# In the last group of an attention kernel, the extra norm tile's statistics move one unit up and its modulation and low part one unit down

## The reference

```
sa, ca, ga, sb, cb, gb = mod            # rows of silu(c) @ wmod; |ga| and |gb| at least 0.25
h = layernorm(x) * (1 + ca) + sa
x1 = x + ga * attention(h)              # 32 q heads, 8 kv heads of 128, rope, causal, window of 128
h = layernorm(x1) * (1 + cb) + sb
out = x1 + gb * ((silu(h @ w1.T + b1) * (h @ w2.T + b2)) @ w3.T + b3)
```

## Time and profile before

| | us |
|---|---|
| median of 3 runs | 1498.3 |
| profiled execution | 1499.11 |
| its span | 1497.3 |
| TensorE busy | 1474.5 (98%) |
| VectorE busy | 1102.8 (74%) |
| GpSimd busy | 863.2 (58%) |
| ScalarE busy | 823.0 (55%) |

### The profile page before, as it was taken

The page is one execution under the profiler, slowest core; times in us unless marked ns, Lnnn a source line. Parts: engine busy times, 40 slices in busy tenths (PEclk is TensorE's granted clock), DMA queues, the critical chain, the costliest instruction groups (busy, mean ns, idle before and its releaser), DMA issues.

```text
span 1497.3 us, 27356 instructions
## 1 busy us (share of the span) xinstructions
PE 1474.5 (98%) x7589; PEld 1227.1 (82%) x7589; DVE 1102.8 (74%) x1852; ACT 823.0 (55%) x2183; POOL 863.2 (58%) x887
## 2 busy tenths in 40 slices
PE   7899999999999999999999999999999999999999
PEld 4578888888888888888888888888888888877887
DVE  6687786877787878788787878787877868783542
ACT  3465655656555656555565655565665556552331
POOL 2356466656565556669855646655664665676333
PEclk9999999999999999999999999999999999999999
DMA  9011110110201111324302020111111101153001
GB/s 317 21 37 57 36 56 28 38 53 7 84 7 56 35 56 35 127 62 128 99 27 66 7 82 9 56 35 56 35 56 35 56 28 35 64 183 127 28 29 57
DMA packets 99216, 90.20 MB, mean 60 GB/s; under 512 B 5466, under 2 KB 73314, under 8 KB 99174
## 3 DMA queue, kind: packets, MB, share of 16 engines
q1 hardware_dynamic: 98582, 88.50, 18.8%
q10 hardware_dynamic: 432, 0.66, 0.1%
q0 software_dynamic: 160, 0.52, 0.1%
HBM read 74.98 MB, written 14.69 MB: 60 GB/s over the span
## 4 chain that ended last, share of the span: by engine, by line
PE 91%; DVE 4%; POOL 2%; issue 1%; ACT 1%; DMA 0%; DVEq 0%; POOLq 0%; ACTq 0%
PE pP L276 11%; PE pP L278 11%; PE pP L277 11%; PE pOp L276 8%; PE pOp L278 8%; PE pOp L277 8%; PE pS L278 4%; PE pS L277 4%; PE pAv L276 4%; PE pS L276 4%; PE pAv L278 4%; PE pAv L277 4%; PE pTr L286 3%; PE pXx L355 1%; POOL pm L1256 1%
## 5 line engine op out<-in xcount | busy, mean ns | idle before, releaser
L1256 POOL TENSOR_SCALAR_AFFINE_SELECT pm<-pT 128x512 fp32r<-128x512 f32 x480 | 393.3, 852 | 474.4 <-DVE pT L868 474.2
L276 PE MATMUL pP<-hT,wp 128*128 128x512 f32 (+1 forms) x776 | 315.1, 406 | 4.7 <-DVE hT L1001 4.0
L278 PE MATMUL pP<-hT,wp 128*128 128x512 f32 (+1 forms) x776 | 303.7, 391 | 0.0
L277 PE MATMUL pP<-hT,wp 128*128 128x512 f32 (+1 forms) x776 | 302.8, 390 | 0.0
L630 ACT CAST oT<-pAv 128x512 fp32r<-128x512 f32 x128 | 74.8, 585 | 280.9 <-PE pAv L278 280.9
L1269 POOL TENSOR_TENSOR rB<-rB,tab 128x512 f32<-128x512 f32 x160 | 218.4, 1377 | 17.3 <-ACT rB L653 17.3
L642 ACT ACTIVATE pr<-pS,nb 128x128 f32<-128x128 f32 x512 | 181.4, 371 | 64.3 <-DVE nb L888 64.3
L898 DVE TENSOR_TENSOR rA<-pP,tab 128x512 f32<-128x512 f32 x160 | 110.2, 689 | 130.8 <-ACT rB L653 130.8
L276 PE MATMUL pOp<-wos,oT 128*128 128x512 f32 x512 | 201.4, 393 | 4.0 <-DVE oT L863 3.8
L278 PE MATMUL pOp<-wos,oT 128*128 128x512 f32 x512 | 199.5, 390 | 0.0
L277 PE MATMUL pOp<-wos,oT 128*128 128x512 f32 x512 | 199.4, 389 | 0.0
(11 more groups left out here) (196 smaller groups left out, 3008.6 us busy)
## 6 DMA issues: line engine op xcount, KB each, us to landing
st<-in_L_attn_wq_dram SPq DMA_DIRECT2D x64, 256.0 KB, 3.6
st<-in_L_attn_wo_dram SPq DMA_DIRECT2D x64, 256.0 KB, 3.8
h_dram<-hs SPq DMA_DIRECT2D x16, 512.0 KB, 3.9
st<-in_L_attn_wk_dram SPq DMA_DIRECT2D x16, 256.0 KB, 4.0
st<-in_L_attn_wv_dram SPq DMA_DIRECT2D x16, 256.0 KB, 2.8
wm<-in_L_wmod_dram SPq DMA_DIRECT2D x4, 1024.0 KB, 10.1
xin<-in_L_attn_x_dram SPq DMA_DIRECT2D x16, 256.0 KB, 3.0
qT<-h_dram SPq DMA_DIRECT2D x2, 2048.0 KB, 10.2
```

Source lines behind the costliest of these rows:

```text
L276: nc.tensor.matmul(o, hi_l, hi_r, start=start, stop=False, skip_group_check=True)
L277: nc.tensor.matmul(o, hi_l, lo_r, start=False, stop=False, skip_group_check=True)
L278: return nc.tensor.matmul(o, lo_l, hi_r, start=False, stop=stop, skip_group_check=True)
L1256: last = nc.gpsimd.affine_select(out=pm[:, own, part], in_=pT[:, part], compare_op=op, fill=0.0, base=0, pattern=[[0, G], [sign, P]], chan ...
```

## The change

In the last group of batch 1 alone, `side_stats`, `side_rstd` and `side_apply` run in unit 3 and not in unit 4; `side_act` and `side_lo` run in unit 7 and not in unit 6. `side_transpose` stays at the end of unit 5. All other groups keep their order.

```diff
@@ act (ScalarE)
                     unit_step(f, u, b, jobs, split=b == 0)
-                    if u == 6:
+                    if u == (7 if b else 6):
                         side_act(f, b)
@@ dve (VectorE)
-            def unit_step(f, u, b, jobs, late=lambda: None, prev=True, prev2=True, split=True):
+            def unit_step(f, u, b, jobs, late=lambda: None, prev=True, prev2=True, split=True, norm=(4, 6)):
...
-                if u == 4:
+                if u == norm[0]:
                     side_stats(f)
...
-                if u == 4:
+                if u == norm[0]:
                     side_apply(f)
-                if u == 6:
+                if u == norm[1]:
                     side_lo(f)
...
-                    unit_step(f, u, b, jobs, late, split=b == 0)
+                    unit_step(f, u, b, jobs, late, split=b == 0, norm=(3, 7) if b else (4, 6))
@@ pool (GpSimd)
-            def unit_step(f, u, b, jobs, prev=True):
+            def unit_step(f, u, b, jobs, prev=True, norm=4):
...
-                if u == 4:
+                if u == norm:
                     side_rstd(f)
...
-                    unit_step(f, u, b, jobs)
+                    unit_step(f, u, b, jobs, norm=3 if b else 4)
```

## The result

The changed kernel took 1500.73 us, the median of 20 runs (1499.34 to 1501.86), against 1498.12 for the kernel before (20 runs, 1496.82 to 1499.68). The ratio is 1.0018, with a 95% interval of 1.0012 to 1.0024: a loss of 2.6 us, small but clear of no change. (The kernel before took 1498.12 us beside the changed one, against 1498.3 in the three runs named at the top.) The profiled execution has a span of 1499.6 us (before 1497.3) and a mean granted clock of 0.995 (before 0.997).

A forecast was written before the change was run, and what follows sets the result against it. TensorE, 91% of the chain, was taken as the bound. Units 4 to 7 summed to -0.3 us, replaced by +0.7 at the first feed-forward transposes: 1499.8 profiled, 1499.0 as median, range 1497.0 to 1501.3.

The forecast's parts named there:

- rival C: Surcharges: GpSimd's multiply ahead of side_lo (1.25), store taking 4.8 (0.9 more); x of tile 14 at 1370.0; total 1501.2; chance 0.12.
- Unit 3 and 4: Added VectorE work in unit 3 makes result_lo(2) and the output projection of unit 4 1.84 us late.
- rival A: In unit 3 side_apply is not held up and takes 0.54 us, not 1.60; total 1498.0; chance 0.13.
- Unit 5: The 1.18 us wait ahead of the output projection goes, leaving TensorE 0.6 us late.
- rival D: Unit 4's late start is not given back in unit 5; TensorE enters unit 6 1.84 late; total 1500.2; chance 0.13.
- Unit 7: Output projection starts at 1345.58 instead of 1345.89, so TensorE is 0.3 us ahead of before.
- The train: SP's late store delays the loads behind it: x of tile 14 lands at 1367.9, ln_rstd(8) starts 0.7 us later.
- Rival B: x of tile 14 does not bind, so only -0.3 stays; total 1498.0; chance 0.12.
- the last one: After the first feed-forward transposes TensorE has few gaps, so their 0.7 us delay stays to the end.
- each microsecond beyond costs one: Each microsecond by which x of tile 14 lands after 1366.9 costs one microsecond.
- Stretch A: From the first score matmul of unit 4 to the first feed-forward transposes (L363); 0.7 us longer was forecast.
- stretch B: From the first L363 to the second, behind the feed-forward wait; no added time was forecast.

The follow-up runs named there:

- e8: Kernel before, with only SP's last store of hs held until the y add of unit 7; 1500.90 us, ratio to before 1.0018.
- e1: Changed kernel, with x of tile 14 loaded ahead of the last hs store and x of tile 15 ahead of the second qT load; 1497.75 us.
- e4: Changed kernel plus 11 unused matmuls on TensorE in the wait ahead of the first feed-forward transposes; 1499.34 us, ratio to before 1.0009.
- e9: Changed kernel plus 4 unused matmuls ahead of the first feed-forward transposes, filling part of the wait; 1500.12 us, ratio to before 1.0014.
- e10: Kernel before with only the statistics and rstd moved to unit 3; 1497.68 us against 1497.63 for before.
- e3: Lower half of the change alone: against the kernel before, only side_act and side_lo move to unit 7; 1500.24 us, ratio 1.0016.
- e2: Upper half of the change alone: against the kernel before, only statistics, rstd and apply move to unit 3; 1498.43 us, ratio 1.0001.
- e6: Kernel before with side_act and side_lo in unit 7, and the x loads of tiles 14 and 15 issued earlier as in e1; 1497.35 us, ratio 0.9993.
- e11: Kernel before plus 6 unused matmuls in TensorE's wait ahead of the output projection in unit 7; 1497.96 us, ratio 0.9999.

## Why the prediction was right about the wait and too small in its size

The forecast was 1499.0 in a range of 1497.0 to 1501.3; 1500.73 lies within, and the way was right. The loss was forecast as 0.7 us and is 2.6. That the range reaches so far is in part luck: its upper end is rival C's, and C's reasons for it didn't come.

- Unit 3 and 4. `side_apply` was foreseen at 1316.8 with 1.60 and took 1.51 from 1316.32, so rival A (0.54) fell. `result_lo(2)` was foreseen 1.84 us late against TensorE; measured from the first scores of unit 4 it is 1.63 late (1319.60 - 1314.33 against 3.64). The wait of near 1.8 us that was named as a sign came as 1.19, with 0.32 more ahead of the second weight transpose, which the prediction had at no cost.
- Unit 5. The wait went, as forecast, with 4.36 us from the first score matmul to the output projection for 4.39; that was rival D's doubt, and D fell.
- Unit 7. 0.96 us of wait is left, for about 1.1 forecast. TensorE entered the feed-forward about 1.0 us earlier than before, 0.5 of it by the stretches; 0.3 was forecast.
- The train. Store landed in 4.1 (3.9 taken), x of tile 14 at 1368.1 (1367.9), add at 1368.13 (1367.95), `ln_rstd(8)` at 1379.20 (1379.2), transposes at 1381.40 (1381.4). That the times agree so closely is in part luck, since unit 4 began 0.45 us earlier here. Counted from there the transposes came at 67.07 us, and the forecast has 66.62 (1381.4 - 1314.78). The load of x of tile 14 took 12.0 us and not the 11.2 of before, why is not shown; the other terms of the train came out a little shorter. e8 shows that this train alone makes the whole loss, e1 that without it none is left. Rival B (x not binding) fell. Rival C had the right total by a wrong way: neither of its two surcharges came.
- The step that failed is the last one: "After that the gaps of TensorE are few, so 0.7 stays to the end." It counted the longer wait by its length only and had nothing for what follows it. So had rival C's "each microsecond beyond costs one". Stretch A was 1.15 us longer, where 0.7 was forecast, and stretch B 1.61 us, where nothing was: there TensorE ran at the lower clock behind the wait. 1.15 + 1.61 = 2.8 against the 2.6 of the medians. e4 shows that the 1.6 hangs on the wait being idle and not on the lateness: filled with matmuls, it leaves A at 0.8 over before and B at 8.63. Its median lies 1.3 over before, with 1.3 to either side.

## What to carry to other kernels

Moving a step on a compute engine also moves the DMA that waits for it, and with it every DMA that the same engine issues later: list what stands there and who uses it with no slack. Small loads that are needed first belong ahead of a store that waits. Price a longer TensorE wait by its length and by what the lower clock behind it may cost: here some 1.3 to 1.6 us more, in 41 of the 42 executions of the three versions whose profiles show a wait of 2.46 to 2.76 us, in 5 of 11 (e9), 4 of 11 (e10) and 6 of 108 (the kernel before) with one of 1.87 or 1.88, in none of the profiles with 1.19 or less.

## What the runs showed of the hardware that was not expected

- Behind waits of 2.46, 2.73 and 2.76 us the granted clock fell from 2.4 to 1.2 GHz in every profile (e8, the changed kernel, e3), and by the mean clock in 41 of their 42 executions; the 24 matmuls behind them took 1.6 us longer in the changed kernel, though only some eight of them ran at the lower level. Behind waits of 0.96 to 1.19 it did in no profile. Waits of 1.86 and 1.87 us in unit 7 left it full in the profiles of before, e2 and e8; one of 1.88 there (e10) and one of 1.87 at L363 (e9) dropped it. The mean clocks on record say the same of all executions: 5 of 11 in e9, 4 of 11 in e10, 6 of 108 in the kernel before. What decides between these is not shown. TensorE had been busy without a break for over 25 us ahead of the waits at L363.
- At the lower level the rows have 0.43 us from start to start of 512-column matmuls. The Trainium skill (TensorE: Matmul & The Clock Gate, section Back-to-back issue gap) puts it at 512 columns over 1.2 GHz, 0.427 us; the trace agrees.
- Which of VectorE and GpSimd holds up the other: `side_apply` took 1.51 us where GpSimd's multiply had started 0.06 us earlier, and 0.65 where VectorE was 0.33 us ahead (the multiply then took 1.48 for 1.28). The Trainium skill (SBUF — State Buffer, section SBUF: two separate sides) says that whoever starts first holds the shared ports for a whole instruction, if VectorE's runs in a two-port mode or has two SBUF inputs; which mode `side_apply` ran in is not shown. The order in these two agrees. The sizes do only in part: in the second, GpSimd lost 0.2 us of the 0.32 that VectorE still ran, and VectorE took 0.11 more than its 0.54. The row of before, in which VectorE started 0.03 us ahead and took 1.60, does not agree, and it is no accident of one record: e3, e6, e8 and e11 have the same lead and 1.60 or 1.61. So to start 0.03 us ahead, by the records, did not keep VectorE's instruction short.
